# Row-by-row fetch of one chunk in every second turn of layers 2 and 3, the last bias in the tail, scatter windows of 144 columns

## The reference

```python
h = relu(layernorm(x))
for l in range(2):                       # layers 0 and 1, with edge attributes
    agg = segment_sum(relu(h[src] + edge_attr), dst, 6250)
    ...                                  # two products with batch norm between
x = x + h
h = relu(layernorm(x))
h = relu(gin(h, w1a, b1a, w1b, b1b))     # layer 2
x = x + gin(h, w2a, b2a, w2b, b2b)       # layer 3
# gin: agg = segment_sum(h[src], dst, 6250); relu(((1 + eps) * h + agg) @ wA.T + bA) @ wB.T + bB
```

## Time and profile before

| what | value |
|---|---|
| median of three runs | 2726.07 us (2722.8 to 2729.74) |
| the profiled execution | 2727.45 us, span 2725.6 us |
| mean granted TensorE clock | 0.853 |
| PE busy | 1897.0 us (70%) |
| DVE busy | 1696.3 us (62%) |
| ACT busy | 737.3 us (27%) |
| POOL busy | 1923.3 us (71%) |

### The profile page before, as it was taken

How to read it: one execution, slowest core, us unless ns; L and a number is a source line. 1 busy time by engine, 2 the same in 40 slices (tenths; PEclk the granted TensorE clock), 3 DMA queues, 4 the chain that set the end, 5 groups by cost and what they waited for, 6 DMA issues and landing times.

```text
span 2725.6 us, 41558 instructions
## 1 busy us (share of the span) xinstructions
PE 1897.0 (70%) x9399; PEld 1275.4 (47%) x9399; DVE 1696.3 (62%) x2880; ACT 737.3 (27%) x1002; POOL 1923.3 (71%) x2024
## 2 busy tenths in 40 slices
PE   3476656556656662656666666566669999899999
PEld 2354444444444442434443444344445656556566
DVE  7798777767677753767777777676773222342213
ACT  4132222222223251333333333334361000310001
POOL 6777777777777727777777777777707777377774
PEclk8688877877778886878888888887889999999999
DMA  6344434443444333444445454455426666365653
GB/s 200 98 131 123 131 108 117 122 129 117 134 118 137 121 111 101 136 137 130 151 130 154 134 158 148 154 150 164 132 92 219 196 202 216 118 213 194 204 180 117
DMA packets 234068, 397.26 MB, mean 146 GB/s; under 512 B 45864, under 2 KB 138876, under 8 KB 233860
## 3 DMA queue, kind: packets, MB, share of 16 engines
q0 software_dynamic: 64256, 131.72, 18.5%
q10 hardware_dynamic: 68192, 146.09, 15.1%
q1 hardware_dynamic: 101412, 117.28, 13.3%
HBM read 333.11 MB, written 61.81 MB: 145 GB/s over the span
## 4 chain that ended last, share of the span: by engine, by line
POOL 48%; PE 24%; issue 17%; DVE 7%; DMA 2%; ACT 1%; DVEq 1%; POOLq 0%; ACTq 0%; SPq 0%
POOL xg L672 47%; PE psA L1536 16%; PE psG L1551 4%; PE psG L1600 2%; DVE cell_room L1116 2%; PE psA L1608 1%; DMA xg<-node_table,src_all 1%; POOL xg L692 1%; DVE xp_room L1130 1%; DVE hid L1076 1%; DVEq L1051 0%; DVE acc L1029 0%; PE psG L1509 0%; PE psG L1630 0%; DVE hid L1246 0%
## 5 line engine op out<-in xcount | busy, mean ns | idle before, releaser
L672 POOL DMA_INDIRECT xg<-node_table,src_all x1496 | 1418.3, 948 | 500.8 <-issue 454.7
L1509 PE MATMUL psG<-hid,xp_room 128*128 128x160 f32 x3072 | 608.0, 373 | 450.9 <-DVE hid L1076 438.3
L1509 PEld LDWEIGHTS psG<-hid,xp_room 128*128 128x128 f32 x3072 | 589.5, 253 | 492.1 <-issue 478.9
L1493 PE MATMUL psA<-cell_room,xp_room 128*128 128x512 f16 (+1 forms) x2336 | 544.8, 386 | 259.5 <-ACT count_out L739 251.0
L1116 DVE TENSOR_SCALAR cell_room<-psG,cell_all 128x932 f16<-128x932 int16 x1088 | 684.0, 686 | 0.0
L692 POOL DMA_INDIRECT xg<-node_table,idx x480 | 469.0, 977 | 249.5 <-issue 247.4
L758 ACT COPY psG<-xp_room 128x512 f32<-128x512 f32 x384 | 226.3, 589 | 1240.0 <-DVE xp_room L1130 992.8
L1493 PEld LDWEIGHTS psA<-cell_room,xp_room 128*128 128x128 f16 x2336 | 231.1, 103 | 538.8 <-ACT count_out L739 285.2
L1130 DVE TENSOR_TENSOR xp_room<-psG,xg 128x512 f32<-128x512 f32 x374 | 252.2, 674 | 361.1 <-DMA xg<-node_table,src_all 325.7
L1029 DVE TENSOR_TENSOR acc<-acc,row_slot 128x38 f32 x192 | 38.7, 202 | 387.6 <-ACT row_slot L837 362.9
L1076 DVE SCALAR_TENSOR_TENSOR hid<-loc_all,round_off,psG 128x2560 f32<-128x2560 f32 x96 | 274.7, 2862 | 0.2
(11 more groups left out here) (156 smaller groups left out, 808.3 us busy)
## 6 DMA issues: line engine op xcount, KB each, us to landing
xp_room<-in_edge_attr_dram ACTq DMA_DIRECT2D x95, 768.0 KB
cell_room<-count_store SPq DMA_DIRECT2D x16, 2850.0 KB
count_store<-count_out ACTq DMA_DIRECT2D x96, 465.5 KB
hid<-count_store SPq DMA_DIRECT2D x16, 2736.0 KB
row_slot<-node_table SPq DMA_DIRECT2D x1888, 0.5 KB
hid<-node_table SPq DMA_DIRECT2D x1888, 0.5 KB
xp_room<-in_edge_attr_dram ACTq DMA_DIRECT2D x95, 256.0 KB
xg<-node_table,src_all POOLq DMA_INDIRECT x1496
```

What stands on the lines that cost most here:

```text
L672: nc.gpsimd.indirect_dma_start(xg[:, n % XG, u, j, :], None, x if n < RAW_TURNS else table, bass.IndirectOffsetOnAxis(ap=src_all[:, s, j:j ...
L1493: last = nc.tensor.matmul(psA[:, bank, 0:w], src_hot[:, hots(n) % 2, at, :], cells[:, c % CELL_RING, c0:c0 + w], start=first, stop=end)
L1509: last = nc.tensor.matmul(psG[:, q, h * WIN:(h + 1) * WIN], ea[:, t, u, j, :], rows[:, u, j, :], start=(u == slots[0] and j == 0), stop=(u ...
```

## The change

Three things. The last chunk (u = 3, j = 3) of every odd turn of layers 2 and 3 is no longer gathered by POOL; 64 of its 128 rows are fetched by SP and 64 by ACT, 512 bytes each, in runs of 16 with their addresses loaded into registers. Their list is loaded by SP near the end of layer 1 into a part of `xg` that is free by then and is shifted to byte offsets by DVE. Both loops begin only when the table of the layer is written. PE waits for the rows ahead of the last chunk's matmul. The last bias is added in the tail, group by group, two groups ahead. `WIN` is 144 in place of 160.

```diff
-WIN = 160
+WIN = 144
+LATE_TURN = 1
+LATE_SLOT = (SLOTS - 1, EPP - 1)
+LATE_PARTS = 8
+LATE_ROWS = P // LATE_PARTS
+SYNC_PARTS = ((0, 1), (2, 3))
+ACT_PARTS = ((4, 5), (6, 7))
...
+            def late_rows(layer, k, parts):
+                sp.wait_ge(reduced[LATE_TURN], sp.snap((k + uses_before(layer, LATE_TURN, pairs)) * rounds + 1))
+                start = sp.snap(k * LATE_ROWS + skipped * (LATE_ROWS // 2)).with_bounds(
+                    min_val=0, max_val=(LATE_PAIRS - 1) * LATE_ROWS)
+                u, j = LATE_SLOT
+                for part in parts:
+                    _, rows = nc.values_load_multi_w_load_instructions(
+                        late_list[part:part + 1, bass.DynSlice(start, LATE_ROWS)], [mybir.EngineType.SP], min_val=0,
...
+                    for i, row in enumerate(rows):
+                        r = part * LATE_ROWS + i
+                        sp.dma_start(xg[r:r + 1, LATE_TURN, u, j, :].bitcast(U8), row_bytes(row)
+                                     ).then_inc(late_landed[part], 16)
             def load_counts(layer):
                 sp.wait_ge(parts_ready, (layer - 1) * NSPLIT)
                 load_half(layer, 0, 1)
+                sp.wait_ge(table_written, 16 * GROUPS * (layer + 1))
+                sp.wait_ge(late_scaled, 1)
                 with sp.Fori(0, pairs) as k:
                     load_half(layer, k + 1, 0)
+                    late_rows(layer, k, SYNC_PARTS[0])
                     load_half(layer, k + 1, 1)
+                    late_rows(layer, k, SYNC_PARTS[1])
...
                     for u in range(SLOTS):
                         for j in range(EPP):
+                            if q == LATE_TURN and (u, j) == LATE_SLOT:
+                                continue
                             nc.gpsimd.indirect_dma_start(
...
+                act.wait_ge(table_written, 16 * GROUPS * (layer + 1))
+                act.wait_ge(late_scaled, 1)
                 before = act.snap(adds_before(layer, pairs, rounds) + 0 * rounds)
                 product_out(0, before)
                 with act.Fori(0, pairs) as k:
+                    late_rows(k, ACT_PARTS[0])
                     next_indices(k, 0)
+                    late_rows(k, ACT_PARTS[1])
                     next_indices(k, 1)
                     product_out(k + 1, act.snap(k * pair_adds(rounds) + rounds * WINDOWS + UPG + before))
...
-                if layer == 3:
-                    nc.vector.tensor_tensor(rows_x[:, :, :], rows_x[:, :, :],
-                                            bias_last[:, :].unsqueeze(1).broadcast_to((P, BLOCKS, D)),
-                                            ALU.add).then_inc(bias_added, 1)
...
+                    for g in range(LAG):
+                        add_bias(g)
                     for g in range(GROUPS):
+                        if g + LAG < GROUPS:
+                            add_bias(g + LAG)
                         b0, nb = g * GB, len(group_blocks(g))
+                        dve.wait_ge(bias_added, g + 1)
                         dve.wait_ge(second_done, layer * LG + g + 1)
...
                         for u in slots:
                             for j in range(EPP):
+                                if q == LATE_TURN and (u, j) == LATE_SLOT:
+                                    for part in range(LATE_PARTS):
+                                        pe.wait_ge(late_landed[part], pe.snap((uses + 1) * (16 * LATE_ROWS)))
                                 last = nc.tensor.matmul(
```

## The result

The changed kernel takes 2880.85 us (median of four runs, 2877.94 to 2884.86), the kernel before 2724.68 beside it (2722.8 to 2729.74): a ratio of 1.057, interval 1.0558 to 1.0582. It is slower by 156 us, where 2842 us, slower by 116, was forecast. The two profiled executions stand 157.4 us apart (2884.86 and 2727.45; the spans 2883.0 and 2725.6).

A forecast was written before the change was run, and what follows sets the result against it. POOL's gathers bound layers 0 and 1, PE layers 2 and 3. Rounds of 46.8 us added 62.0 and 55.2, windows took 0.9: 2727.45 became 2843.8, set at 2842 us against the three-run median; range 2780 to 2910.

The forecast's parts named there:

- the ring: Layers 2 and 3: product copy, ACT's 64 rows, landing, last chunk, 72 count matmuls, next copy; 46.8 us a round; chance 0.70.
- Rival (a): Layers 2 and 3: ACT's rows land within 22.2 us of the copy, PE stays the bound, 2706 us; chance 0.09.
- (b): Layers 2 and 3: PE's wait is about 1 us a round, paid for by shorter windows; no change; chance 0.04.
- the landing: Layers 2 and 3: time for the last row to arrive after issue, taken as 2.0 us, bounds 0 and 5.99.
- Rival (d): Layers 2 and 3: row DMAs wait among count-load packets, landing 6 us for 2, +56 us, 2898; chance 0.07.
- The issue term: Layers 2 and 3: ACT issues 64 rows with register loads at 0.416 us each, 26.6 us a round.
- The clock term: Layers 2 and 3: PE runs at half clock after each wait for rows, losing 2.3 us a round.
- Rival (c): Layers 2 and 3: SP and ACT hold each other up while issuing, +3.7 us a round, 2894 us; chance 0.10.
- The 6.8 us of the bias: Layer 3: its seven rounds lasted 6.8 us longer than layer 2's because the DVE bias addition held one gather.
- The windows: Layers 2 and 3: 144 columns shorten only the last window of each layer, -0.9 us for both.
- the list and the waits ahead of the loops: Ahead of the loops: list load, DVE shift and extra waits fall into existing waits, costing 0, at most 1 us.
- The quick end of the ring: Layers 2 and 3: quickest rows and landing without clock loss, a round of 41.4 us, 2765 us in all.

The follow-up runs named there:

- the first experiment: The changed kernel with ACT issuing its first 32 rows ahead of the product copy and the other 32 behind the even turn's index copy: 2723.82 us, ratio 0.9992.
- the last experiment: The changed kernel with ACT's order as in the first experiment and 48 of SP's rows ahead of its second count load, 16 behind: 2711.51 us, ratio 0.995.

## Why the prediction was right, and where its size was off

**The mechanism held.** The forecast was a ring through ACT: the rows begin behind the product copy, PE waits for them, and the copy waits for PE. The profile after shows each link, and the first experiment opens the ring by moving one call and gives all 157 us back. Rival (a), rows hidden, falls for this order of ACT's queue, as does (b). Rows that are nearly hidden do come near to the 2706 of (a): 2711.51 in the last experiment's order and 2707.87 with SP's rows alone.

**Its terms**, in the round that starts with the copy at T = 2084.13:

| term | forecast | after |
|---|---|---|
| last ACT row issued | T + 27.5 | T + 28.3 |
| its landing | 2.0 | 3.5 |
| PE goes on (its wait) | T + 29.5 (7.3) | T + 31.9 (9.8) |
| last chunk, 72 counts, to the copy | 17.3 | 17.7 |
| round | 46.8 | 49.6 |

Over 14 rounds the mean is (346.27 + 344.04) / 14 = 49.3, so 2.5 us a round or 35 us in all were missing. The term that was mis-sized most is the landing. It was taken from a 256 KB store (2.4 us) as a small transfer; counted from the end of the issue, a row takes 1.2 with no count load beside it (layer 3's last round) and 3.5 beside one, and 2.0 lies between. The right row to weigh was the gather of 5.99 us beside a count load, which stood there as the upper bound. Rival (d) had the loads as the cause, with 4 us a round in place of the 1.5 measured; the run with small loads shows that the loads make the landing longer (it is 3.5 to 4.1 us with them and 1.5 without). The issue term, 0.416 us per row from SP's long stretch, came out right for the rows (12.64 us per 32 with a register load inside it, 0.395 each); what it lacked is 0.8 us, within the 1.57 from the copy to the first row and the 1.83 between the batches.

**The clock term held**: 2.3 us per wait were forecast. In the chain the 72 count matmuls behind a wait take 15.6 to 17.0 us over the 14 rounds, 16.3 in the mean, for 14.52, and the last two matmuls of the window 0.82 for the 0.48 of the first experiment: 2.1 more in all. The granted clock is 0.50 in the stretch from 2116 to 2121 and 1.00 again from 2122 in the round above.

**Rival (c) falls.** Beside SP's rows a batch of ACT takes 12.64 us, without them 12.48; the full price would have been 3.7 us a round. The trace shows no more than 0.2 us per 32 rows of ACT, so the measurement decides against two engines that take turns.

**The 6.8 us of the bias** were put to the held gather, with PE's later wait of 3.83 us and a granted clock of 0.50 behind it, and rightly so: with the bias in the tail alone layer 3 is 6.9 us shorter and the tail no longer. **The windows** were forecast at -0.9 us for both layers, in the last window of each. The tail behind the last copy is 32.05 us against 31.96, so nothing of it is seen; and on the kernel before the narrower window is no gain at all (1.0017), since POOL becomes late sooner. Rival (a) counted its 12.9 us as a gain with POOL relieved of a gather, which is the condition that makes it one.

**The rest.** POOL not late, SP's second load not late, layers 0 and 1 as before, SP done ahead of ACT: all as forecast. The 4.3 us ahead of layer 2, where the list and the waits ahead of the loops were put at 0, at most 1, lie within what the other runs show there. The quick end of the ring was added up wrongly: its own terms give 40.9 us (0.5 + 25.0 + 0.4, then 0.4 + 14.5 + 0.1), not 41.4; the range does not reach down to either.

**Left open.** Why the landing grows from under 4 us to 6 and 8 when SP's rows behind a load go out together with ACT's last. Four cases are shown: 1.5 us without a load; 3.5 to 4.4 for a row issued some 9 us behind the load, whose bytes move until 2114 in the round above (287 GB/s from 2112.40 to 2114.00, 66 in the next 2 us), so that the row lands 2 us behind them; 5.7 to 8.3 with many rows of SP and ACT behind a load that has already been moved (5.7 and 8.1 in the last round of layer 3, in which no other load runs); and a landing just short enough for PE not to wait when most of SP's rows go ahead of the load. That the full loads lengthen the landing is shown by the run with small ones. Whether a row waits behind packets of the load on the same DMA engines, behind the other rows, or for something else was not separated.

## What to carry to other kernels

When an engine that issues DMAs also does a small step for the consumer of those DMAs, write out its queue over two rounds and look for a ring: here one 0.54 us copy behind 64 issues cost 157 us, and moving it ahead of half of them cost nothing. Price many small DMAs per row with their register loads (0.395 us each here), and the landing of the last by the transfers beside it and ahead of it, not by its own size: the same 512 bytes took 1.5 to 8.3 us. Before shortening a step, check how much lead the next engine has: windows of 144 alone gave a ratio of 1.0017 here, since POOL became late sooner.

## What the runs showed of the hardware

From the beginning of its issue a 512-byte row takes 1.5 us to land with no count load beside it, 3.8 in the mean when it is issued some 9 us behind a load of 2850 KB, and 5.7 to 8.3 as the last of many rows of SP and ACT that went out behind a load of 2736 KB. SP and ACT issuing rows side by side hardly slow each other: in the change 32 rows, one register load of 16 included, take 12.0 us on SP and 12.6 on ACT, against 11.98 for SP in the run without ACT's rows and 12.48 for ACT in the run without SP's; the most was SP's 13.26 in the first experiment. A bias addition of 6.67 us on DVE that held one gather of POOL (7.45 us for 0.94) cost 6.9 us at the end of the layer, though POOL had a lead when it happened.
